# Marking an edge item's rows with a float32 comparison in place of a bf16 one, in a graph layer on one Trainium2 core

## The reference

```python
def _L0_gnn_ref(features, indices, ...):
    h = features @ W_layer.T + b_layer
    a1 = (h @ w_a1.T + b_a1)[:, 0]
    a2 = (h @ w_a2.T + b_a2)[:, 0]
    row, col = indices[0], indices[1]
    v = leaky_relu(a1[row] + a2[col], negative_slope=0.01)
    m = segment_max(v, row, num_segments=n)
    ev = exp(v - m[row])
    s = segment_sum(ev, row, num_segments=n)
    att = ev / s[row]
    return segment_sum(att[:, None] * h[col], row, num_segments=n)

xn = _layernorm(x, axis=-1)
x = x + _L0_gnn_ref(xn, edge_index, ...) + _L0_mix_ref(xn[None], ...)[0]
x = x + _L0_ffn_ref(_layernorm(x, axis=-1)[None], ...)[0]
```

## Time and profile before

| | before |
|---|---|
| median of 3 runs | 1750.54 us |
| the profiled execution, its own time | 1749.8 us |
| its span | 1748.1 us |
| busy: PE, PEld, DVE, ACT, POOL | 80%, 64%, 77%, 38%, 65% of the span |
| mean granted TensorE clock | 0.911 of 2.4 GHz |

### The profile page before, as it was taken

One profiled execution on the slowest core, in us unless ns is written; L12 is line 12 of the kernel. 1 busy time (PEld: TensorE's weight loads), 2 busy tenths in 40 slices (PEclk: granted clock), 3 DMA queues, 4 the chain that ended last, 5 costly groups with the idle time before them and its releaser, 6 DMA issues. The chain is left out here.

```text
span 1748.1 us, 27650 instructions
## 1 busy us (share of the span) xinstructions
PE 1404.9 (80%) x8473; PEld 1110.3 (64%) x8473; DVE 1341.2 (77%) x4033; ACT 663.4 (38%) x1867; POOL 1131.9 (65%) x1196
## 2 busy tenths in 40 slices
PE   5449888883588788888888888888888888887699
PEld 3337777762476666666666667766666666664487
DVE  8898999993497777777777878887777777784244
ACT  0014334330254444444444544444444444441000
POOL 0038888885777777777777777777777777740000
PEclk8769999996599999999999989899999989998599
DMA  9601111111344444444444444444444444520822
GB/s 115 125 11 57 45 51 54 49 51 40 104 117 119 119 122 120 118 120 118 121 117 119 125 117 120 119 112 121 119 121 120 119 121 120 145 68 21 294 74 74
DMA packets 118355, 180.11 MB, mean 103 GB/s; under 512 B 41727, under 2 KB 90238, under 8 KB 118207
## 3 DMA queue, kind: packets, MB, share of 16 engines
q0 software_dynamic: 44384, 113.26, 24.8%
q1 hardware_dynamic: 62735, 45.22, 11.6%
q10 hardware_dynamic: 11088, 19.87, 3.1%
HBM read 142.98 MB, written 35.29 MB: 102 GB/s over the span
## 5 line engine op out<-in xcount | busy, mean ns | idle before, releaser
L1036 POOL DMA_INDIRECT big<-node_table,rest x850 | 857.1, 1008 | 243.9 <-issue 230.3
L1107 PE MATMUL psum<-big 128*125 128x257 f32 x1700 | 433.9, 413 | 80.7 <-DVE big L1606 80.7
L1107 PEld LDWEIGHTS psum<-big 128*125 128x125 f32 x1700 | 341.6, 206 | 145.3 <-DVE big L1606 87.6
L1255 ACT ACTIVATE rest<-big,rest 128x125 f32<-128x125 bf16 x850 | 267.6, 489 | 149.5 <-DVE rest L1554 149.5
L337 POOL DMA_INDIRECT edge_groups<-rest x112 | 139.8, 1248 | 77.6 <-DVE rest L755 49.8
L1606 DVE TENSOR_SCALAR big<-big,rest 128x125 f32<-128x125 bf16 x850 | 171.9, 290 | 0.0
L1561 DVE TENSOR_REDUCE rest<-rest 128x125 f32<-128x2125 f32 x50 | 118.3, 2367 | 32.1 <-ACT rest L1255 32.1
L1135 PE MATMUL psum<-rest,big 125*128 125x126 f32 x416 | 71.2, 324 | 69.5 <-DVE big L1525 69.4
L1246 ACT COPY big<-psum 125x1024 bf16<-125x1024 bf16 x150 | 103.8, 763 | 37.0 <-PE psum L1084 37.0
L1135 PEld LDWEIGHTS psum<-rest,big 125*128 125x128 f32 x416 | 60.6, 224 | 88.4 <-DVE big L1525 87.3
L1142 PE MATMUL psum<-big 125*128 125x256 f32 x416 | 101.3, 387 | 0.0
(11 more groups left out here) (390 smaller groups left out, 2711.7 us busy)
## 6 DMA issues: line engine op xcount, KB each, us to landing
big<-node_table,rest POOLq DMA_INDIRECT x850, 2.8
slice_weights<-rest ACTq DMA_DIRECT2D x52, 252.0 KB, 2.7
big<-slice_weights ACTq DMA_DIRECT2D x25, 252.0 KB, 7.4
big<-slice_weights SPq DMA_DIRECT2D x25, 252.0 KB, 7.4
node_table<-big SPq DMA_DIRECT2D x50, 126.0 KB
normalised_turned<-big SPq DMA_DIRECT2D x50, 125.0 KB, 2.3
rest<-normalised_turned SPq DMA_DIRECT2D x50, 125.0 KB, 2.4
out_dram<-rest SPq DMA_DIRECT2D x50, 125.0 KB
```

The lines of the kernel that those rows point to most:

```text
L1036: pool.indirect_dma_start(Gt[:, u, q * TW:(q + 1) * TW], None, table, bass.IndirectOffsetOnAxis(ap=item[:, u, 2 * q:2 * q + 1], axis=0)).t ...
L1107: mm = pe.matmul(bank[bAgg][0:R, 0:D + 1], P[:, u, q, :], Gt[:, u, q * TW:q * TW + D + 1], start=q == 0, stop=q == Q - 1)
L1255: act.activation(V[:, :, q], O[:, u, q, 0:R], ACT.Copy, scale=score[:, u, q:q + 1]).then_inc(s_v, 1)
```

## The change

The row numbers of the edges are copied as float32, once each (17 values in place of 17 pairs), and compared with the float32 `iota_r`. `row_id` is gone, and a `nop` stands where it was made, so that the semaphore count stays. `O` stays bf16, with the same values. The order of the engines' work stays the same.

```diff
-            local = a.take(128, Q, 2, dtype=BF16)
-            row_id = a.take(128, RP, dtype=BF16)
+            local = a.take(128, Q)
...
-                    dve.tensor_copy(row_id, iota_r[:, 1:RP + 1]).then_inc(s_fin, 1)
+                    dve.nop().then_inc(s_fin, 1)
...
-                        dve.tensor_copy(local, item[:, u, :].rearrange("p (q w) -> p q w", w=2)[:, :, 1:2].to_broadcast(
-                            [128, Q, 2])).then_inc(s_local, 1)
+                        dve.tensor_copy(local, item[:, u, :].rearrange("p (q w) -> p q w", w=2)[:, :, 1]).then_inc(s_local, 1)
                         dve.wait_ge(s_local, i + 1)
-                        dve.tensor_tensor(O[:, u].rearrange("p q (a b) -> p q a b", b=2),
-                                          row_id.rearrange("p (a b) -> p a b", b=2).unsqueeze(1).to_broadcast(
-                                              [128, Q, RP // 2, 2]),
-                                          local.unsqueeze(2).to_broadcast([128, Q, RP // 2, 2]),
-                                          ALU.is_equal).then_inc(s_rows, 1)
+                        dve.tensor_tensor(O[:, u], iota_r[:, 1:RP + 1].unsqueeze(1).to_broadcast([128, Q, RP]),
+                                          local.unsqueeze(2).to_broadcast([128, Q, RP]), ALU.is_equal).then_inc(s_rows, 1)
```

## The result

The changed kernel takes 1808.78 us, the median of 4 runs (1806.62 to 1812.14), against 1750.57 (1749.77 to 1753.2) for runs of the kernel before beside it: a ratio of 1.0335, 95% interval 1.032 to 1.035, so 58 us slower. The profiled execution took 1806.62 us with a span of 1804.9, 56.8 more than before. The forecast was 1805.0, 1797 to 1815.

The account below looks back on a forecast made before the run. POOL's back-to-back gathers bound the loop, without slack. 50 x (1.11 for the longer comparison - 0.02 for the copy) = +54.5 us on the 1748.1 span gives 1802.6, profiled 1804.3, median 1805.0; range 1797 to 1815.

Parts of the forecast that it names:

- POOL sets the loop's pace, and gathers are held to the comparison's end: Item loop: POOL waits for no other engine; a gather meeting L1542 ends 0.82 us after it, 29.3 us lost in all.
- the fourth step: Loop after the comparison: POOL and DVE continue at the same distance, nothing absorbs the loss, DVE's L1554 wait stays about 87 us.
- rival A: Gathers beside L1542: POOL's stall doesn't grow, DVE's wait absorbs its 1.1 us an item; about 1750.5 us, chance 5%.
- The comparison takes 2385 ns: L1542, 50 times: with float32 inputs it goes from 1276 to 2385 ns, +1.11 us an item.
- Rival D: Comparison L1542: float32 inputs run at the pace of bf16 ones, so no slowing; about 1750 us, chance 2%.
- POOL loses 1.11 us more in every item: Gather meeting L1542: let go at that instruction's end, which moves by 1.11 us, whatever the item's phase.
- The late-marked item: Item whose L1542 ends before the next gather needs its access: loss 0.03 us before, about 1.15 forecast.
- the early-marked one: Item whose L1542 comes early against the gathers and holds one: loss 0.93 us before, 2.04 forecast.
- From there both engines go on as before: After the comparison: last gather, landing, L1554 and its wait keep their distance; nothing absorbs POOL's loss, DVE's wait about 87 us.
- Rival C: Item phases change for the worse: slow low-clock stretches vanish, every item takes 22.83 us, 20.6 us on top; 1825.6, chance 5%.
- The copy takes 171 ns and costs nothing: Copy to `local`, 50 times: 17 fewer elements, from 189 to 171 ns, -0.02 us an item; no gather held.
- the upper bound's mechanism: Copy to `local`: the cast might hold a gather as L1542 does, up to 0.19 us an item, 9.5 us.

Follow-up runs that it names:

- pairs_again: The kernel before with each item's bf16 comparison in two instructions (8 and 9 of the 17 columns): 1736.89 us beside 1751.47, ratio 0.9925.
- late_again: The kernel before plus one unused single-input reduction (918 elements) behind each item's bf16 comparison: 1768.15 us beside 1751.47, ratio 1.0073.

## Why the prediction was right, and where it wasn't

*POOL sets the loop's pace, and gathers are held to the comparison's end.* The second half is right, the first only just (see the fourth step). Gathers beside the comparison end 0.81 to 0.84 us after it in the changed kernel as well, at lengths from 1.99 to 3.12 us; pairs_again turned the mechanism round and gained 14.6 us. The inference of the Trainium skill, page "SBUF — State Buffer", section "Who interferes with whom", that a tensor_tensor does not stall descriptor generation, does not foretell these gathers; rival A is out with it. The runs do not tell whether what is held is the generation or the gather's reading of its node numbers, which lie in SBUF in `item`, and with the second the section's sentence on two SBUF inputs, which the prediction set against that inference, agrees.

*The comparison takes 2385 ns.* 2393. Rival D is out.

*POOL loses 1.11 us more in every item.* The comparison's stalls grew by 88.1 - 29.4 = 58.7 us, 1.17 an item, for 55.5 forecast. The late-marked item went to 1.16 (the gather of 2.11) where 1.15 was forecast, the early-marked one to 1.99 where 2.04 was. Early-marked items have become the rule, 36 of 50 (gathers of 2.9 us and more) in place of 25 (1.8 and more), which is the surplus.

*From there both engines go on as before.* This step failed. Stalls beside the slice softmax's division fell from 12.5 to 2.0 us, a gain of 10.5 that was not in the sum; and DVE's wait for the last gather, which was to stay at 87 us and to tell the forecast from A (35), went to 3.9. By that sign the forecast was wrong, though its time was right. DVE's slack is gone: from the nine-column scores to the next comparison took 9.8 us or 11.4 before, and takes 11.5 to 13.2 in nearly all items after (12.76 in the item shown, from 907.29 to the comparison at 920.05), and the stretch from the comparison to those scores went from 9.85 without its wait (1016.33 - 3.10 - 1003.38 in the earlier trace rows) to 10.84 (907.29 - 896.45). In the stretch behind those scores PE is now the busy one. This is the item shown, behind them and in front of them:

```profile
907.30:919.70 12.40, 12.40 (x61) 10.39 (x60) 8.08 (x28) 4.87 (x15) 9.48 (x12) 0.87 0.47 125
896.50:907.20 10.70, 7.47 (x53) 5.30 (x53) 10.39 (x37) 6.04 (x15) 8.78 (x8) 0.83 0.37 94
```

PE is busy for all of the first 12.40 us and idle for 3.2 of the 10.70 behind the comparison, and ACT's copy of the slice weights, which needs PE, comes late. PE's longest waits for DVE inside the loop, before and then after, counted over the whole span:

```profile
PE psum L1107 <- DVE big L1606: 80.7, 50, 2.3
PE psum L1135 <- DVE big L1525: 69.4, 37, 5.0
...
PE psum L1160 <- DVE rest L1453: 25.2, 48, 1.9
```

```profile
PE psum L1159 <- DVE rest L1452: 83.1, 49, 3.0
PE psum L1106 <- DVE big L1601: 68.8, 50, 2.2
...
PE psum L1134 <- DVE big L1524: 8.9, 2, 5.0
```

PE's standing has moved to one place behind the comparison, but there is not more of it: 186.7 us of the loop before (1120.90 - 934.18), 171.2 after (1171.70 - 1000.50). Its busy time grew by 66.3 us instead, as the granted clock of the loop fell from 0.93 to 0.85. That lateness of DVE lowers the clock is shown by late_again, where nothing else was changed (0.865 to 0.884 against 0.907 to 0.915). By which step it does so, and why it falls further in the changed kernel, is open; the new place of the standing is a guess.

From the first comparison to the last an item takes 23.34 us, against POOL's 23.43 (1171.7 over 50). In the items 2 to 39 (counted from 0) DVE waits for no gather, and POOL for nobody: two chains side by side. DVE begins there 7.56 us behind the last gather's end and is 2.66 behind it at the end, since its items take 23.31 us and POOL's 23.45. The forecast's picture, DVE led by POOL's gathers, fits only in the items 40 to 45, where DVE is 1.9 us behind them again with waits of about 0.5. So POOL's stream is the longer one by a hair, and by these numbers DVE's chain would have taken over had the stalls grown by less, as it did in late_again. There it took 22.18 us an item over the same items in the profiled, fast execution, so lateness at that clock doesn't give the 23.31 by itself.

*Rival C* named the right thing, the granted clock, and the wrong direction. The granted clock changed the pattern of the items, but there are not fewer slow stretches, there are more, and the cost lay in DVE's slack rather than in the phases. The reason given against it, that PE would idle more, did not come true either: it idles 15.5 us less and the clock is lower all the same.

*The copy takes 171 ns and costs nothing.* It takes 232 in the mean. It is the upper bound's mechanism from the other side: DVE waits for POOL here. It is a small term in time, 2 us in all against the 189 of before, but it lets many comparisons start 0.03 us after a gather's end, the phase in which the next gather loses 1.99.

*The sum.* 54.5 forecast for the span, 56.8 measured: +58.7 at the comparison, -10.5 at the division, +1.0 at other places, +1.6 between POOL's gathers, +3.6 before the loop and +2.4 behind it. All but the first were forecast as zero. The 3.6 are no effect that I can name: the first gather starts between 431.2 and 435.4 us in the traces of the two kernels, late_again and pairs_again. The 2.4 are DVE's lost slack, since in the last item it comes to the nine-column scores 5.19 us after the last gather, where it was 2.72. So the total was nearer than its parts, which is partly luck: a gain at the division that nobody forecast made up for the surplus at the comparison and the growth outside the loop, and POOL's stream just stayed the longer of the two.

*What stays open.* How much of the 58 us the hold would cost with no lateness, and the reverse, in the changed kernel. late_again gives 0 to 29 us for lateness alone, pairs_again shows that stalls are paid in full while POOL is last; the runs that were to part the two in the float32 kernel came where the other bound hides both. What lowers the granted clock is open as well.

## What to carry to other kernels

Where GpSimd issues gathers back to back, as here, an instruction of VectorE with two SBUF inputs can cost time though VectorE itself has slack: the gather that meets it loses the time from 0.13 us after its own start to that instruction's end. Ask of each such instruction how long it is. Cutting one in two helped here, because a gather held by the first half is let go before the second ends: 12.9 us of stalls in place of 29.4. Check how much slack the second engine really has before you call a delay covered. 2.1 us an item looked like cover for 1.1, but with VectorE later TensorE's granted clock fell too, and the slack was gone. And compare versions within one group of runs on the same chip only.

## What the runs showed of the hardware that I had not expected

- An indirect DMA's instruction on GpSimd takes 0.947 us alone; met by a comparison or division with two SBUF inputs, it ends 0.81 to 0.84 us after that one, whether inputs are bf16 or float32. A reduction with one input, of 1.10 or 2.37 us, leaves it within a few hundredths of its length.
- A cast of 17 int32 words to 17 float32 that begins about 0.64 us into such a gather lasts until the gather's end (0.30 us in place of 0.17), while a cast of 34 with each word read twice takes 0.19 there.
- One instruction of 1.10 us more on VectorE in each item, and nothing else changed, lowered TensorE's mean granted clock from 0.907 to 0.915 down to 0.865 to 0.884 (late_again).
- The same kernel took 1751 us in some groups of runs and 2358 to 2388 on other chips, with gaps of up to 2.1 us between TensorE's small matmuls and waits of up to 16 us in front of ACT's copy of PE's transposes, whose end the profile doesn't name. On one of these, a version that differs from the changed kernel in the copy alone took 2067. The cause was not found.
